# Two diagonal blocks of a Gram matrix packed in one fp32 matrix: narrower low-part products and a scaled split

## The chip, the core and the metric

One kernel runs on one core of a Trainium2 chip. The metric is the device time of one execution in microseconds (us). A core has a matrix engine (TensorE, PE in the profile), a vector engine (DVE), a scalar engine (ACT), GpSimd (POOL) and a sync engine (SP) that here only issues DMAs. Each runs its own instruction list in order; they wait for one another on semaphores.

## The reference, cut to what matters

```
text_p  = x @ W_text + b_text            # x: 4 x 2048 x 512
audio_p = ctx @ W_audio + b_audio        # ctx: 4 x 77 x 384
Q = layer_norm(text_p, g1, beta1);  K = layer_norm(audio_p, g2, beta2)
alpha = softmax(Q @ K^T / sqrt(512))
h = alpha @ audio_p @ W_out + b_out
out = layer_norm(h + x, g_out, beta_out)
```

`Q` is never formed. The scores need `x` times a matrix of 77 columns, and the variance of each row of `text_p`, which is a quadratic form `x G x^T` with the Gram matrix `G` = `W_text` (centred) times its transpose. `G` is symmetric, so only its upper block triangle is kept: block row k (128 rows) has 512 - 128k columns, with everything right of the diagonal block doubled.

## The kernel before

**Precision.** Each fp32 product that has to be exact is made of three fp32r products: high x high, high x low, low x high (`parts3`, L1080). A high part is a value rounded to fp32r, a low part the rest. `proj_hi` and `proj_lo` hold both parts of the projection matrix, once for each of 4 batches: per block row k the Gram columns, then 80 columns that are not Gram (77 scores, a linear term, a mean, one spare). The widths per block row are 592, 464, 336 and 208.

**Steps.** The 8192 rows of `x` go in 32 steps of 256 rows; step s takes batch s % 4, and each step has two tiles t = 0, 1 of 128 rows. The loops are written out on DVE, ACT and POOL, and PE and SP have the first steps written out. The PE body of a step (L1284) is: transpose tile 0 of this step into `psT`; mix tile 0 of three steps ago; project tile 0 of the previous step; mix tile 1; transpose tile 1; project tile 1, with the transposes of the probabilities in its midst. `project` (L1247) issues 3 products of 208 columns (L1258), then, at L1268, 3 of 464 (k = 1), 3 of 384 (k = 0), 3 of 336 (k = 2) and 3 of 208 (k = 3). `psT` is a single buffer: ACT rounds it to `x_hi` (L574), DVE subtracts to get `x_lo` (L806), and the next transpose waits for `x_lo_ready`. DVE's list in a step is: scores and quadratic form of tile 1 of the previous step (L908, L909), `stat_eps`, `hid` of tile 0, `x_lo` of tile 0, logits, maximum, scores and quadratic form of tile 0, `parts`, `hid` of tile 1, `x_lo` of tile 1, `inv_sum`, `sc_part`.

**Before the steps.** PE makes block row k of G in a PSUM bank (`gram`, L1125). ACT takes the high part (`t_hi`, L523), DVE the low part (`t_lo`, L767), for batch 0 only. SP copies them to batches 1 to 3 with two DMAs for each block row (`copy_gram`, L300). The same SP list then loads `x` of steps 2 and 3, places the values in `wo_hi` and `wo_lo` with 21 small SBUF-to-SBUF copies (L335), and only behind these loads `x` of step 4, whose wait is for `hid` of step 0 (L324 to L326). The second step of projections (PE body 2) is the first that waits for all Gram copies (`t_copied`, L1251).

Of the kernel before, what the change touches and what calls it, by code (L numbers as in the profile page):

```python
# [25 lines left out]
ALU = mybir.AluOpType  # L26
# [7 lines left out]
def cross_attention(nc, x, ctx, w_text, b_text, w_audio, b_audio, w_out, b_out,  # L34
# [33 lines left out]
    with ExitStack() as stack:  # L68
# [78 lines left out]

        room = [zs[:].rearrange("p b t h -> p (b t h)"), hid[:].rearrange("p c t h -> p (c t h)")]
# [14 lines left out]
        mean_of = borrow(1, P)  # L163
        mean_r = kg_hi[:, 0, 0:P]
# [34 lines left out]
        wo_hi_ready, wo_ready = sem("wo_hi_ready"), sem("wo_ready")  # L199
        val_placed = [sem(f"val_placed{q}") for q in range(B)]  # L200
# [87 lines left out]
        def _(sp):  # L288
# [84 lines left out]
        def _(pool):  # L373
# [6 lines left out]
                                    pattern=[[-1, P]], channel_multiplier=1).then_inc(ident_ready, 1)  # L380
            nc.gpsimd.memset(score_c[:, :, S:SC], 0.0).then_inc(extras_ready, 1)
# [9 lines left out]
            for k in range(KD):  # L391
                at = NX_AT[k]
                nc.gpsimd.memset(f32(proj_hi[:, :, at:at + 1]), -1.0 / D).then_inc(extras_ready, 1)
# [6 lines left out]

            pool.wait_ge(kvar_ready, 1)
# [3 lines left out]
            pool.wait_ge(extras_ready, 4 + KD)  # L405
            for k in range(KD):
                at = LIN_AT[k]
                nc.gpsimd.tensor_copy(proj_hi[:, :, at], lin[:, k:k + 1].to_broadcast([P, B])).then_inc(lin_hi_ready, 1)
            pool.wait_ge(lin_hi_ready, KD)
            for k in range(KD):  # L410
                at = LIN_AT[k]
                nc.gpsimd.tensor_tensor(proj_lo[:, :, at], lin[:, k:k + 1].to_broadcast([P, B]),
# [72 lines left out]
        def _(act):  # L485
# [34 lines left out]
            for k in range(KA):  # L520
                act.wait_ge(cxT_psum, k + 1)
                nc.scalar.activation(cxT[:, k, :], V_BANK[k][:, 0:BS], ACT.Copy).then_inc(cxT_ready, 1)
            def t_hi(k):  # L523
# [22 lines left out]
            t_hi(1)  # L546
# [5 lines left out]
            for k in range(2, KD):  # L552
                t_hi(k)
# [22 lines left out]
            def score_hi(k):  # L576
                act.wait_ge(m_psum, k + 1)
                nc.scalar.activation(proj_hi[:, :, SCORE_AT[k]:SCORE_AT[k] + S],
                                     M_BANK[k][:, 0:BS].rearrange("p (b s) -> p b s", b=B), ACT.Copy).then_inc(m_hi, 1)
# [146 lines left out]
        def _(dve):  # L726
# [40 lines left out]
            def t_lo(k):  # L767
                dve.wait_ge(g_hi, k + 1)
# [31 lines left out]
            t_lo(1)  # L800
# [22 lines left out]
            for k in range(2, KD):  # L823
                t_lo(k)
            linear(KD - 1)
            dve.wait_ge(krstd_ready, 1)
# [22 lines left out]

            dve.wait_ge(bo_loaded, 16)  # L850
# [36 lines left out]
            score_lo(3)  # L887
# [479 lines left out]
```

## Time and profile before

| what | value |
|---|---|
| median of 3 runs | 277.38 us (276.97 to 277.71) |
| the profiled execution: its own time | 277.88 us |
| its span, first to last instruction | 276.2 us |
| PE busy | 264.3 us, 96% |
| DVE busy | 230.8 us, 84% |
| POOL busy | 203.4 us, 74% |
| ACT busy | 199.1 us, 72% |
| granted TensorE clock, mean over the span | 0.992 |

The 1.7 us between the span and the time of the profiled execution lie around the first and the last instruction. Busy matmul time overlaps from one matmul to the next; the pace of PE is read from start to start.

### The profile page before, as it was taken

What the parts mean: (1) busy time and instruction counts of PE and PEld (TensorE: products, weight loads), DVE (VectorE), ACT (ScalarE), POOL (GpSimd) and SP (SyncE); (2) the same over time, 40 slices, a digit from 0 to 9 for tenths busy, and PEclk for the clock granted to TensorE, in tenths of its full rate; (3) what the DMA queues carried; (4) which work ended last, traced back from release to release, by engine and by line L of the source; (5) the groups of instructions that cost most, each with busy time, mean ns of one, the idle gap of its engine ahead of it and who ended that gap; (6) DMA issues with size and microseconds to landing.
All of it is one profiled execution on the core that took longest, in us unless ns stands there. A gap on an engine that the chain in (4) does not pass through costs nothing.

```text
span 276.2 us, 5994 instructions
## 1 busy us (share of the span) xinstructions
PE 264.3 (96%) x1705; PEld 240.3 (87%) x1705; DVE 230.8 (84%) x716; ACT 199.1 (72%) x509; POOL 203.4 (74%) x223
## 2 busy tenths in 40 slices
PE   6799999999999999999999999999999999999980
PEld 6579788999999999999999999999999999999830
DVE  3757889788888888888888888888888888888895
ACT  3584293257888887777777778888888888888881
POOL 5053400113699999999999999999999999999985
PEclk9999999999999999999999999999999999999996
DMA  6919794432244444444444444444444444454116
GB/s 188 285 53 303 277 345 159 120 105 77 77 154 152 157 152 153 154 152 153 152 153 152 152 152 153 153 152 152 152 152 154 153 152 152 152 153 148 81 77 266
DMA packets 21056, 44.03 MB, mean 159 GB/s; under 512 B 2114, under 2 KB 4750, under 8 KB 21034
## 3 DMA queue, kind: packets, MB, share of 16 engines
q1 hardware_dynamic: 20410, 42.74, 45.8%
q10 hardware_dynamic: 624, 1.06, 1.4%
q14 instruction: 16, 0.13, 0.2%
q8 instruction: 6, 0.10, 0.1%
HBM read 21.19 MB, written 16.78 MB: 138 GB/s over the span
## 4 chain that ended last, share of the span: by engine, by line
PE 86%; DVE 4%; DMA 3%; POOL 3%; ACT 2%; issue 1%; SPq 1%; POOLq 0%; ACTq 0%; DVEq 0%
PE psY L1268 44%; PE psO L1280 10%; PE psT L1193 10%; PE psY L1258 7%; DMA zs<-in_ctx_dram 3%; PE psE L1243 2%; PE psE L1244 2%; PE psY L1098 2%; PE psY L1162 1%; PE psT L1131 1%; PE psT L1162 1%; POOL zs L464 1%; POOL zs L460 1%; POOL rstd L452 1%; PE psY L1131 1%
## 5 line engine op out<-in xcount | busy, mean ns | idle before, releaser
L1268 PE MATMUL psY<-proj_hi,x_hi 128*128 128x464 f32 (+3 forms) x256 | 86.1, 336 | 0.0
L1268 PE MATMUL psY<-proj_hi,x_lo 128*128 128x464 f32 (+3 forms) x256 | 83.2, 325 | 0.0
L1268 PE MATMUL psY<-proj_lo,x_hi 128*128 128x464 f32 (+3 forms) x256 | 83.1, 325 | 0.0
L429 POOL TENSOR_TENSOR zs<-zs,shift 128x512 f32<-128x512 f32 x55 | 70.9, 1289 | 4.3
L423 POOL TENSOR_TENSOR zs<-zs,gain 128x512 f32<-128x512 f32 x55 | 71.3, 1296 | 0.9 <-ACT zs L616 0.9
L605 ACT ACTIVATE waste_act<-hid,sc 128x512 bf16<-128x512 f32 x60 | 43.4, 723 | 38.8 <-DVE hid L929 38.8
L435 POOL TENSOR_TENSOR rstd<-stat_eps,neg_half 128x4 f32<-128x4 f32 x30 | 30.5, 1017 | 40.6 <-DVE stat_eps L921 40.6
L1268 PEld LDWEIGHTS psY<-proj_lo,x_hi 128*128 128x128 f32 x256 | 48.5, 189 | 1.5
L1268 PEld LDWEIGHTS psY<-proj_hi,x_lo 128*128 128x128 f32 x256 | 48.3, 189 | 1.6
L1268 PEld LDWEIGHTS psY<-proj_hi,x_hi 128*128 128x128 f32 x256 | 48.4, 189 | 1.5
L909 DVE CUSTOM_DVE_ANT_0 waste_dve<-psY,xs,sums 128x514 bf16<-128x514 f32 x64 | 47.7, 745 | 0.2 <-issue 0.2
L616 ACT ACTIVATE zs<-hid,shift,rstd 128x512 f32<-128x512 f32 x59 | 47.5, 805 | 0.0
L929 DVE SCALAR_TENSOR_TENSOR hid<-psO,inv_sum,xs 128x512 f32<-128x512 f32 x60 | 44.8, 747 | 0.0
L806 DVE TENSOR_TENSOR x_lo<-psT,x_hi 128x512 fp32r<-128x512 f32 x64 | 43.6, 682 | 0.9 <-ACT x_hi L574 0.7
L574 ACT ACTIVATE x_hi<-psT 128x512 fp32r<-128x512 f32 x64 | 37.7, 589 | 6.7 <-PE psT L1193 6.7
L1193 PE MATMUL psT<-ident,xs 128*128 128x128 f32 x256 | 38.6, 273 | 0.0
L1193 PEld LDWEIGHTS psT<-ident,xs 128*128 128x128 f32 x256 | 29.9, 141 | 4.5 <-issue 0.4
L908 DVE TENSOR_TENSOR sc<-psY,sc_part 128x78 f32<-128x78 f32 x64 | 15.4, 240 | 21.4 <-PE psY L1268 18.1
L1280 PE MATMUL psO<-wo_hi,parts_t 128*128 128x512 f32 x60 | 26.9, 448 | 0.1
L1280 PE MATMUL psO<-wo_lo,parts_t 103*128 103x512 f32 x60 | 23.6, 394 | 0.0
L625 ACT ACTIVATE psD<-logits,neg_max 128x77 f32<-128x77 f32 x62 | 19.2, 309 | 2.2 <-DVE neg_max L941 2.2
L1258 PE MATMUL psY<-proj_hi,x_hi 128*128 128x208 f32 x64 | 19.3, 301 | 0.0
(230 smaller groups left out, 484.4 us busy)
## 6 DMA issues: line engine op xcount, KB each, us to landing
xs<-in_x_dram SPq DMA_DIRECT2D x64, 256.0 KB, 3.0
out_dram<-zs SPq DMA_DIRECT2D x29, 512.0 KB, 3.9
out_dram<-zs SPq DMA_DIRECT2D x6, 256.0 KB, 2.0
xs<-in_L_xattn_W_text_dram SPq DMA_DIRECT2D x4, 256.0 KB, 3.7
xs<-in_L_xattn_W_out_dram SPq DMA_DIRECT2D x2, 512.0 KB, 4.2
wa<-in_L_xattn_W_audio_dram SPq DMA_DIRECT2D x1, 768.0 KB, 7.8
proj_hi<-proj_hi SPq DMA_DIRECT2D x1, 768.0 KB, 8.8
proj_lo<-proj_lo SPq DMA_DIRECT2D x1, 768.0 KB, 10.7
```

The costliest lines, as they stand in the source:

```text
L423: nc.gpsimd.tensor_tensor(zs[:, q, t, :], zs[:, q, t, :], gain[:], ALU.mult).then_inc(zg_ready, 1)
L429: nc.gpsimd.tensor_tensor(zs[:, q, t, :], zs[:, q, t, :], shift[:], ALU.add).then_inc(out_ready, 1)
L574: nc.scalar.activation(x_hi[:, b % 2, t, :], psT[:], ACT.Copy).then_inc(x_hi_ready, 1)
L605: nc.scalar.activation(waste_act[:, t, :], hid[:, (b - 3) % 2, t, :], ACT.Square, bias=sc[:, q, t, S:S + 1], accum_out=stat[:, (b + 1) % B ...
L616: nc.scalar.activation(zs[:, q, t, :], hid[:, b % 2, t, :], ACT.Identity, bias=shift2[:, q, t:t + 1], scale=rstd[:, b, T + t:T + t + 1]).t ...
L806: nc.vector.tensor_tensor(x_lo[:, b % 2, t, :], psT[:], f32(x_hi[:, b % 2, t, :]), ALU.subtract).then_inc(x_lo_ready, 1)
L909: nc.vector.tensor_tensor_reduce(out=waste_dve[:, t, 0:QUAD_W], in0=psY[:, t, QUAD_AT:QUAD_AT + QUAD_W], in1=xs_rows[:, q, t, X_AT - 1:X_A ...
L929: nc.vector.scalar_tensor_tensor(hid[:, (b - 3) % 2, t, :], psO[:], inv_sum[:, q, t:t + 1], xs[:, q, t, :], ALU.mult, ALU.add).then_inc(hi ...
L1193: last = nc.tensor.transpose(psT[:, k * P:(k + 1) * P], xs[:, b, t, k * P:(k + 1) * P], ident[:])
L1258: last = nc.tensor.matmul(psY[:, t, B_AT:512], part[:, par, t, 0:P], w[:, q, 0:SW + P], start=(n == 0), stop=(n == 2))
L1268: last = nc.tensor.matmul(psY[:, t, to:to + n0], part[:, par, t, k * P:(k + 1) * P], w[:, q, at:at + n0], start=(n == 0), stop=(n == len(P ...
L1280: last = nc.tensor.matmul(psO[:], parts_t[0:rows, (b - lag) % 2, t, n, :], v[0:rows, q, :], start=(n == 0), stop=(n == 1))
```

## The change

Block rows 1 and 2 are "packed". The low part of a diagonal block is put below the diagonal of the high part's block (where a symmetric block held a mirror image), so that one 128-column product carries both. The rows are scaled first, by `rs`, so that the diagonal is exactly an fp32r value; `x_lo` of those 128 columns is then `psT * x_scale - x_hi` in place of `psT - x_hi`, and the score, linear and mean columns of block rows 1 and 2 are scaled as well. In `project`, the `x_hi` x `proj_lo` product of block row 1 has 336 columns in place of 464, that of block row 2 has 208 in place of 336.

```
@@ the projection on PE
                     to = 512 + max(k - 1, 0) * P
+                    if k in PACKED and w is proj_lo:
+                        at, n0, to = at + P, n0 - P, to + P
@@ x_lo on DVE
-                nc.vector.tensor_tensor(x_lo[:, b % 2, t, :], psT[:], f32(x_hi[:, b % 2, t, :]),
-                                        ALU.subtract).then_inc(x_lo_ready, 1)
+                nc.vector.tensor_tensor(dst[:, 0:KD:KD - 1, :], src[:, 0:KD:KD - 1, :], high[:, 0:KD:KD - 1, :], ALU.subtract)
+                for k in PACKED:
+                    last = nc.vector.scalar_tensor_tensor(dst[:, k, :], src[:, k, :], x_scale[k], high[:, k, :], ALU.mult, ALU.subtract)
+                last.then_inc(x_lo_ready, 1)
@@ DVE before the steps
+            for n, k in enumerate(PACKED):
+                nc.vector.tensor_tensor_reduce(out=waste_dve[:, n, 0:P], in0=g_raw[k][:, 0:P], in1=ident[:], scale=1.0, scalar=1e-30,
+                                               op0=ALU.mult, op1=ALU.add, accum_out=dd[:, n:n + 1]).then_inc(dg_ready, 1)
...
+            link(nc.vector.reciprocal(rec[:], dd[:]))
+            link(nc.vector.tensor_tensor(rs[:, 0:2], dd[:, 2:4], rec[:, 0:2], ALU.mult))
+            nc.vector.tensor_tensor(rs[:, 2:4], dd[:, 0:2], rec[:, 2:4], ALU.mult)
+            nc.vector.tensor_scalar(rs[:, 4:6], rs[:, 0:2], 2.0, None, ALU.mult)
+            nc.vector.tensor_scalar(rs[:, 6:8], rs[:, 0:2], -1.0 / D, None, ALU.mult).then_inc(rs_ready, 1)
...
+                if k < len(PACKED):
+                    diagonal_rest(k)
+                else:
+                    block_rest(k - len(PACKED))
...
+            dve.wait_ge(pkT_psum, 1)
+            for n, k in enumerate(PACKED):
+                nc.vector.tensor_tensor(proj_hi[:, 0, Y_AT[k]:Y_AT[k] + P], psD[:, n * P:(n + 1) * P], pk_hi[n], ALU.add).then_inc(pack_ready, 1)
@@ PE before the steps
+            pe.wait_ge(pk_ready, len(PACKED))
+            for n in range(len(PACKED)):
+                last = nc.tensor.transpose(psD[:, n * P:(n + 1) * P], pk_lo[n], ident[:])
+            last.then_inc(pkT_psum, 1)
             constant(0, C_BANK)
-            pe.wait_ge(lin_lo_ready, KD)
+            pe.wait_ge(lin_lo_ready, KD + len(PACKED))
+            pe.wait_ge(goff_ready, len(PACKED))
+            pe.wait_ge(pack_ready, len(PACKED))
@@ SP
                         if b == 2:
-                            for k in range(1, KD):
-                                copy_gram(k)
+                            copy_gram(KD - 1)
                             sp.wait_ge(wo_ready, KH)
...
                 if isinstance(i, int) and (i, b) == (0, B - 1):
+                    for k in PACKED:
+                        copy_gram(k)
                     sp.wait_ge(val_psum, len(KEYS))
```

`diagonal_rest` and `block_rest` are each one DVE instruction of 128, 128, 256 and 128 columns with a per-partition scalar. ACT takes a raw copy of block rows 1 and 2 (`g_raw`) in place of their high parts and makes the scaled high parts later, while it waited before; POOL has four more small operations at the start, two products of 128 columns, and four more columns to fill.

The list of SP before, from the loads of step 1 (rows of L326) to the values (L335):

```order
L326 DMA xs<-in_x_dram 128x512 [waits lin_ready]
L326 DMA xs<-in_x_dram 128x512
L305 DMA proj_hi<-proj_hi 128x3x384 [waits g_hi]
L305 DMA proj_lo<-proj_lo 128x3x384 [waits g_lo]
L305 DMA proj_hi<-proj_hi 128x3x256 [waits g_hi]
L305 DMA proj_lo<-proj_lo 128x3x256 [waits g_lo]
L305 DMA proj_hi<-proj_hi 128x3x128 [waits g_hi]
L305 DMA proj_lo<-proj_lo 128x3x128 [waits g_lo]
L326 DMA xs<-in_x_dram 128x512 [waits wo_ready]
L326 DMA xs<-in_x_dram 128x512 x3
L335 DMA wo_hi<-wa 77x512 [waits val_lo_ready,val_hi_ready,val_psum]
```

The same place after the change (the loads of `x` are L343 there, the Gram copies L323, the values L354):

```order
L343 DMA xs<-in_x_dram 128x512 [waits lin_ready]
L343 DMA xs<-in_x_dram 128x512
L323 DMA proj_hi<-proj_hi 128x3x128 [waits g_hi]
L323 DMA proj_lo<-proj_lo 128x3x128 [waits g_lo]
L343 DMA xs<-in_x_dram 128x512 [waits wo_ready]
L343 DMA xs<-in_x_dram 128x512 x3
L323 DMA proj_hi<-proj_hi 128x3x384 [waits pack_ready,goff_ready]
L323 DMA proj_lo<-proj_lo 128x3x256 [waits pack_ready,goff_ready]
L323 DMA proj_hi<-proj_hi 128x3x256 [waits pack_ready,goff_ready]
L323 DMA proj_lo<-proj_lo 128x3x128 [waits pack_ready,goff_ready]
L354 DMA wo_hi<-wa 77x512 [waits val_lo_ready,val_hi_ready,val_psum]
```

Four Gram copies moved behind the loads of steps 2 and 3 and now wait for `pack_ready`; the values, and all that follows them, stand behind that wait.

DVE before the steps, before the change, from `kvar` to the key scales (L828):

```order
L821 TENSOR_SCALAR kvar<-psY 52x1
L770 SCALAR_TENSOR_TENSOR proj_lo<-psD,proj_hi 128x128 [waits g_hi]
L770 SCALAR_TENSOR_TENSOR proj_lo<-psD,proj_hi 128x128
L770 SCALAR_TENSOR_TENSOR proj_lo<-psO,proj_hi 128x128 [waits g_hi]
L786 ISA waste_dve,lin<-xs,bt_rows 128x512
L786 ISA lin 128x1
L828 TENSOR_SCALAR kg_lo<-ident,krstd 128x128 [waits krstd_ready]
```

and after it:

```order
L885 ISA waste_dve,dd<-zs,ident 128x128 [waits g_raw_ready]
L885 ISA dd 128x1
L885 ISA waste_dve,dd<-zs,ident 128x128
L885 ISA dd 128x1
L826 SCALAR_TENSOR_TENSOR proj_lo<-psO,proj_hi 128x128 [waits g_hi]
L842 ISA waste_dve,lin<-xs,bt_rows 128x512
L842 ISA lin 128x1
L891 RECIPROCAL rec<-dd 128x4 [waits dh_ready,dg_ready]
L892 TENSOR_TENSOR rs<-dd,rec 128x2 [waits dve_own]
L893 TENSOR_TENSOR rs<-dd,rec 128x2 [waits dve_own]
L894 TENSOR_SCALAR rs<-rs 128x2
L895 TENSOR_SCALAR rs<-rs 128x2
```

The two low parts of block row 2 are gone from here, and two reductions and five small operations in a chain stand ahead of the key scales.

## Rows read from the trace of the kernel before

**Rows 1.** The page, part 1: busy us, share of the span, instructions.

```profile
PE 264.3 (96%) x1705; PEld 240.3 (87%) x1705; DVE 230.8 (84%) x716; ACT 199.1 (72%) x509; POOL 203.4 (74%) x223
```

**Rows 2.** Timeline, one projection on PE: start us, duration us, engine, line, what.

```profile
154.43 0.39 PE L1268 MATMUL psY<-proj_hi,x_hi 128*128 128x464 f32 x1
...
155.08 0.34 PE L1268 MATMUL psY<-proj_hi,x_hi 128*128 128x384 f32 x1
...
155.61 0.31 PE L1268 MATMUL psY<-proj_hi,x_hi 128*128 128x336 f32 x1
...
156.06 0.26 PE L1268 MATMUL psY<-proj_hi,x_hi 128*128 128x208 f32 x1
...
156.38 0.41 PE L1280 MATMUL psO<-wo_hi,parts_t 128*128 128x512 f32 x1
```

**Rows 3.** Timeline of one step, PE and DVE, from `sc` (L908) to `sc`.

```profile
153.20 0.60 PE L1193 MATMUL psT<-ident,xs 128*128 128x128 f32 x4
...
153.40 0.24 DVE L908 TENSOR_TENSOR sc<-psY,sc_part 128x78 f32<-128x78 f32 x1 [0.62 <-PE psY L1268]
...
155.12 0.68 DVE L806 TENSOR_TENSOR x_lo<-psT,x_hi 128x512 fp32r<-128x512 f32 x1
...
155.71 0.49 DVE L938 SCALAR_TENSOR_TENSOR logits<-sc,rstd,psD 128x77 f32<-128x77 f32 x2
...
158.77 0.68 DVE L806 TENSOR_TENSOR x_lo<-psT,x_hi 128x512 fp32r<-128x512 f32 x1
...
160.22 0.24 DVE L908 TENSOR_TENSOR sc<-psY,sc_part 128x78 f32<-128x78 f32 x1 [0.57 <-PE psY L1268]
```

**Rows 4.** Groups of DVE by form: count, busy us, mean ns of one, idle before.

```profile
L806 DVE TENSOR_TENSOR x_lo<-psT,x_hi 128x512 fp32r<-128x512 f32 x64 | 43.6, 682 | 0.9 <-ACT x_hi L574 0.7
...
L946 DVE RECIPROCAL inv_sum<-prob_sum 128x2 f32<-128x2 f32 x30 | 4.7, 156 | 0.0
...
L863 DVE TENSOR_TENSOR proj_lo<-psY,proj_hi 128x308 fp32r<-128x308 f32 x3 | 1.4, 458 | 0.0
...
L831 DVE SCALAR_TENSOR_TENSOR kg_lo<-ident,krstd,kg_lo 128x128 fp32r<-128x128 f32 x2 | 0.6, 334 | 0.0
...
L770 DVE SCALAR_TENSOR_TENSOR proj_lo<-psD,proj_hi 128x128 fp32r<-128x128 f32 x2 | 0.5, 273 | 0.0
```

**Rows 5.** Timeline of DVE before the first steps.

```profile
30.16 0.63 DVE L828 TENSOR_SCALAR kg_lo<-ident,krstd 128x128 fp32r<-128x128 f32 x3
...
45.96 0.46 DVE L863 TENSOR_TENSOR proj_lo<-psY,proj_hi 128x308 fp32r<-128x308 f32 x1
```

**Rows 6.** Timeline of PE: tile 0 transposed (steps 1, 4), second step's first projection.

```profile
45.54 0.66 PE L1193 MATMUL psT<-ident,xs 128*128 128x128 f32 x4
...
52.07 0.34 PE L1258 MATMUL psY<-proj_hi,x_hi 128*128 128x208 f32 x1
...
64.38 0.60 PE L1193 MATMUL psT<-ident,xs 128*128 128x128 f32 x4
```

**Rows 7.** Timeline of SP's list: start us, time of the issue us, line.

```profile
40.79 1.72 SPq L335 DMA_DIRECT2D wo_hi<-wa  x2
...
57.59 0.74 SPq L335 DMA_DIRECT2D wo_lo<-zs  x1
59.58 13.99 SPq L326 DMA_DIRECT2D xs<-in_x_dram  x5
```

**Rows 8.** Gram copies (L305): ns of an issue min/median/max; landing.

```profile
L305 SPq DMA_DIRECT2D proj_hi<-proj_hi x4: 606/987/1347, 20.6 to 35.1; - x4
...
DMA to landing us min/median/max: 3.6/5.1/10.7
```

**Rows 9.** Value copies (L335): ns of an issue min/median/max.

```profile
L335 SPq DMA_DIRECT2D wo_hi<-wa x11: 652/742/1175, 40.8 to 56.0; - x11
```

**Rows 10.** The page, part 6, loads of x: count, KB, median us to landing.

```profile
xs<-in_x_dram SPq DMA_DIRECT2D x64, 256.0 KB, 3.0
```

**Rows 11.** A stretch at the end: PE, PEld, DVE, ACT, POOL busy; granted clock; DMA.

```profile
270.00:273.00 3.00, 0.00 (x0) 0.00 (x0) 2.73 (x5) 0.69 (x2) 2.56 (x3) 0.75 0.99 391
```

More of the change, by code:

```diff
@@ L163, in cross_attention @@
         mean_of = borrow(1, P)
+        g_raw = {k: borrow(0, D - k * P) for k in PACKED}
+        pk_hi, pk_lo = [borrow(0, P) for _ in PACKED], [borrow(0, P) for _ in PACKED]
+        tri = borrow(1, P)
         mean_r = kg_hi[:, 0, 0:P]
@@ L392, in _ @@
                 at = NX_AT[k]
-                nc.gpsimd.memset(f32(proj_hi[:, :, at:at + 1]), -1.0 / D).then_inc(extras_ready, 1)
+                if k not in PACKED:
+                    nc.gpsimd.memset(f32(proj_hi[:, :, at:at + 1]), -1.0 / D).then_inc(extras_ready, 1)
             def out_lo(k):
@@ L404, in _, with column @@
             pool.wait_ge(lin_ready, KD)
[L405 to L412, printed above, removed]
+            pool.wait_ge(extras_ready, 4 + KD - len(PACKED))
+            pool.wait_ge(rs_ready, 1)
+            nc.gpsimd.tensor_tensor(lin_r[:], lin[:, 1:3], rs[:, 0:2], ALU.mult).then_inc(lin_r_ready, 1)
+            pool.wait_ge(lin_r_ready, 1)
+            def column(k):
+                return lin_r[:, PACKED.index(k):PACKED.index(k) + 1] if k in PACKED else lin[:, k:k + 1]
+            extra_columns = [(LIN_AT[k], column(k)) for k in range(KD)] + [(NX_AT[k], rs[:, 6 + n:7 + n]) for n, k in enumerate(PACKED)]
+            for at, col in extra_columns:
+                nc.gpsimd.tensor_copy(proj_hi[:, :, at], col.to_broadcast([P, B])).then_inc(lin_hi_ready, 1)
+            pool.wait_ge(lin_hi_ready, KD + 2)
+            for at, col in extra_columns:
+                nc.gpsimd.tensor_tensor(proj_lo[:, :, at], col.to_broadcast([P, B]),
                                         f32(proj_hi[:, :, at]), ALU.subtract).then_inc(lin_lo_ready, 1)
@@ L522, in _, with t_raw @@
                 nc.scalar.activation(cxT[:, k, :], V_BANK[k][:, 0:BS], ACT.Copy).then_inc(cxT_ready, 1)
+            def t_raw(k):
+                act.wait_ge(g_psum, k + 1)
+                nc.scalar.activation(g_raw[k], W_BANK[k][:, 0:D - k * P], ACT.Copy).then_inc(g_raw_ready, 1)
             def t_hi(k):
@@ L544, in _ @@
             load_row(shift, beta_out, gs_loaded)
-            t_hi(1)
+            t_raw(1)
             for k in range(KH):
@@ L551, in _ @@
                 nc.scalar.activation(KSQ[k], kT[:, k, :], ACT.Square).then_inc(ksq_ready, 1)
-            for k in range(2, KD):
-                t_hi(k)
+            t_raw(2)
+            t_hi(KD - 1)
+            act.wait_ge(dg_ready, 2)
+            nc.scalar.activation(dd[:, 2:4].bitcast(F32R), dd[:, 0:2], ACT.Copy).then_inc(dh_ready, 1)
+            act.wait_ge(rs_ready, 1)
+            act.wait_ge(pk_own, len(PACKED))
+            for n, k in enumerate(PACKED):
+                nc.scalar.activation(pk_hi[n].bitcast(F32R), pk_lo[n], ACT.Copy, scale=rs[:, 4 + n:5 + n]).then_inc(pk_hi_ready, 1)
+            for n, k in enumerate(PACKED):
+                at, w = Y_AT[k] + P, D - (k + 1) * P
+                nc.scalar.activation(proj_hi[:, 0, at:at + w], g_raw[k][:, P:P + w], ACT.Copy,
+                                     scale=rs[:, 4 + n:5 + n]).then_inc(goff_hi_ready, 1)
             def value_hi(n):
```

67 lines of the change are left out of this document (56 added, 11 removed).

## The prediction, made before the changed kernel ran

> **What bounds the kernel now.** I read the page's shares first: PE is busy 96% of the span, DVE 84%, POOL 74% [rows 1]. That alone says only who is near the limit, so I read one steady step. From one `sc` (L908) to the next are 160.22 - 153.40 = 6.82 us [rows 3]. At both, DVE had sat idle for 0.6 us until PE's projection ended: PE sets the pace, and DVE has 0.57 to 0.62 us of slack in each step. PE's cost by width, start to start [rows 2]: three products of 464 columns take 155.08 - 154.43 = 0.65 us (0.217 each), three of 336 take 0.45 (0.150), three of 208 take 0.32 (0.107).
>
> Before the first step another thing matters. SP issues 21 value copies (L335) one after the other, from 40.79 to 58.33 us, 17.54 us in all [rows 7]; an issue of them occupies SP for 0.74 us in the median and never under 0.65 [rows 9]. At 59.58 us comes the load of `x` for step 4. It lands some 3.0 us later [rows 10], 62.6, and PE transposes it at 64.38 [rows 6]: 1.8 us to spare, and no more. Whatever delays SP's list by over 1.8 us (and is not matched by a delay of PE) stops PE at step 4.
>
> **PE's saving in the steps.** In each tile one product goes from 464 to 336 columns (0.217 - 0.150 = 0.067 us) and one from 336 to 208 (0.043): 0.11 us, from the slope 0.107. I take 0.107, so 0.21 us in a step of two tiles, and 6.61 us a step if nothing else binds.
>
> **DVE's cost in the steps.** `x_lo` was one instruction of 682 ns [rows 4], 0.59 us from its start to the next one's (155.71 - 155.12) [rows 3], so about 0.08 us overlap with the next. Now there are three. The subtract of 256 columns: the slope between 308 and 512 columns is (682 - 458) / 204 = 1.1 ns a column [rows 4], so 0.40 us. The two of 128 columns with a scalar per partition: 273 ns with a constant scalar, 334 ns with one per partition [rows 4]; the second is the nearer form. The sum less three overlaps is 0.40 + 0.67 - 0.24 = 0.83 us, against 0.60: 0.23; I take 0.21 more per tile. The bounds are 0.12 (273 ns each, some rounding) and 0.30 (hardly any overlap). DVE gets 0.42 us more work in a step that becomes 0.21 us shorter, against 0.6 us of slack: nearly full.
>
> Who waits for it? The next transpose (L1193) needs `x_lo` of tile 1, since `psT` is one buffer. This closes a loop over two steps: from `sc` at 153.40, which starts when a projection ends, to the end of the second `x_lo`, 158.77 + 0.68 = 159.45, is 6.05 us; from the start of a transpose of tile 0 (153.20) to the next-but-one `sc` (160.22) is 7.02 us [rows 3]; some 0.05 us (my estimate) for the signal. Before, that is 13.12 us against two steps of PE, 13.64: the loop does not bind. After, it is 13.12 - 0.21 + 2 x 0.21 = 13.33 us, 6.67 a step, above PE's 6.61. So the step costs 6.67 us, and the saving is 0.15 us a step. With 0.12 per tile PE binds and it is 0.21; with 0.30 it is 0.06. The change stops paying in the steps at 0.36 us more per tile.
>
> The Trainium skill ("Perfetto Trace Analysis", Optimizing Scalar/DVE Operations) puts the engine-busy overhead of a DVE instruction that reads PSUM at about 125 ns. By it two more instructions cost 0.25 us per tile and the step 6.71 us, 1.2 us more over the 29 steps counted below; the nearest row here gives the figure above, and both lie inside the bounds.
>
> **What comes before the steps.** All on DVE, whose list there runs nearly without a pause up to `score_lo(3)` (L863 at 45.96) [rows 5].
> - Two reductions of 128 columns and a chain of five small operations replace two low parts ahead of the key scales (L828, at 30.16 before [rows 5]). Two low parts out, two reductions in, some 0.2 us net; the small operations take 156 ns or so each [rows 4], three of them with the wait for the one before, 0.8 us. Key scales and what PE does with them: 1.0 us later.
> - Four instructions among the low parts of `kg`: two hide in DVE's waits for ACT; those of 256 and 128 columns do not: 0.6 us.
> - Two `x_lo` at 0.21 and two scaled score parts at 0.07: 0.56 us. So `score_lo(3)` starts near 45.96 + 2.2 = 48.1.
> - Then two additions of 128 columns (0.4 us): `pack_ready` at 49.0. PE waits for that before its step 1, whose transpose began at 45.54 [rows 6]: 3.5 us later. From both sides: 2.5 (ACT and PE hide part) to 4.2.
>
> I cost ACT's and POOL's new work ahead of the steps at nothing: both engines stand idle there while DVE and PE make the key scales and, for POOL, while the high parts of `wo` are awaited. If that cover went, each would add less than 1 us.
>
> **SP's list, the term that decides.** Before, the Gram copies were issued from 31 us on, and the values from 40.79. Now four Gram copies wait for `pack_ready` at 49.0, and the value copies, and behind these the load for step 4, stand behind them. Four issues at 0.6 to 1.35 us [rows 8], taken as 0.8: 3.2 us, so values from 49.1 + 3.2 = 52.3 on. Plus 17.5 us of value issues: 69.8. Plus 3.0 us for the load: 72.8. PE's transpose of step 4 was at 64.38; it comes **8.4 us** later (7.6 with 0.6 us per Gram issue, 10 with 1.2). The 3.5 us above are inside these 8.4, not beside them. So is the wait of the second step for the last Gram copy: issued at 51.5, landing 3.6 to 5.1 us later [rows 8], 55 to 56.6, against 52.07 + 3.5 - 0.2 = 55.4 [rows 6]. The values themselves are in time: the first batch's four are issued by 55.6 and first used some 60.
>
> PE then stands idle for roughly 5 us at step 4. In a stretch of 3 us at the end without a matmul the granted clock averages 0.75, so it has dropped from 2.4 to 1.2 GHz inside it [rows 11]. How long it stays down once PE works again no row shows. Bounds: nothing, and half a step's worth lost (3.4 us). I take 2.0.
>
> **Sum.** After step 4's transpose 29 pairs of projections remain: 29 x 0.15 = 4.4 us back. 8.4 + 2.0 - 4.4 = +6.0 us. The profiled execution took 277.88 us against the median 277.38; against that median: **283.4 us**.
>
> **Rivals.**
> 1. PE keeps the whole saving (`x_lo` costs under 0.15 us more per tile): 29 x 0.21 = 6.1 back, 8.4 + 2.0 - 6.1 = +4.3, 281.7; without any clock loss 279.7. For it: the loop exceeds PE by 0.06 us only.
> 2. No stop at step 4, and the kernel is faster. Mechanism: an issue holds SP only while the queue behind it is full, so 21 value copies in a quiet stretch go out quickly and the load for step 4 leaves when `hid` of step 0 is ready. It decides if value issues average under about 0.4 us. Then only the 3.5 us remain, less the saving of 31 steps, 4.7: 276.2, or 274.3 with all of PE's saving. Against it: the lowest value issue of all is 0.65 us [rows 9], also in the stretch where little else moved. The Trainium skill ("DMA: Bandwidth & Descriptors", Anatomy of one DMA — SWDGE (gpsimd) path) puts sequencer dispatch at some 50 ns and calls descriptor generation small; that is for another path, but by it this rival would hold. The trace disagrees.
> 3. DVE becomes the bound of the steps (over 0.36 us more per tile, or 13.6 us in the loop of two steps): nothing comes back, 277.4 + 8.4 + 2.0 = 287.8. For it: DVE is nearly full, and small waits can add up. Against it: no row of 128 columns is that dear.
>
> **Chances.** Forecast 0.50; rival 1, 0.27; rival 2, 0.12; rival 3, 0.11. Changes under 0.3% (0.8 us) can't be told from none. Slower by more: 0.87; within: 0.03; faster: 0.10. The range reaches from rival 1 without a clock loss and with the short Gram issues (277.4 + 7.6 - 6.1 = 278.9) to just over rival 3, 288.5; rival 2 is left out.
>
> **What would show it.** In the changed trace: PE idle for about 5 us ahead of L1282 in step 4, released by a DMA of `x`; SP's value issues from about 52 to 70 us; `sc` to `sc` of 6.6 to 6.7 us and DVE's idle time ahead of it nearly gone; a granted clock under 1 after the stop. I am wrong if `x` for step 4 is issued by 64 us, or if the steps take 6.82 us or more.

## The result: 3.5% slower, and the profile after

Over four runs of each kernel the time went from 277.18 us (276.44 to 277.71) to 286.80 us (286.66 to 286.87): a ratio of 1.0348, 95% interval 1.0323 to 1.0374, +9.6 us. The forecast was 283.4 with a range up to 288.5, so the sign and the range held and the middle was 3.4 us short. The profiled execution took 286.85 us with a span of 285.1, 8.9 us longer than before.

Part 1 of the page after, against [rows 1]:

```profile
PE 267.7 (94%) x1707; PEld 240.8 (84%) x1707; DVE 249.4 (87%) x855; ACT 204.2 (72%) x512; POOL 206.9 (73%) x232
```

PE has fewer columns to do and is counted busy for longer: some of it ran at half clock, and in the steady steps the profile counts it as busy all the time in both kernels (68.00 us of the 68 from 174 to 242), though it has less to do in the second. DVE has 139 more instructions and 18.6 us more work.

**Where the time went before the steps were steady.** The timeline of PE after (start us, duration us, engine, line, what), first the transposes of tile 0 and tile 1 of step 1, tile 0 of step 2, then around step 4. The same instructions stood at 45.54, 48.36, 51.66, 64.38, 68.05 and 71.21 before, so [rows 6] and its neighbours shift by +2.50, +3.87, +3.75, +7.46, +8.99 and +8.88 us.

```profile
48.04 0.63 PE L1282 MATMUL psT<-ident,xs 128*128 128x128 f32 x4 [1.52 <-issue]
52.23 0.61 PE L1282 MATMUL psT<-ident,xs 128*128 128x128 f32 x4
55.41 0.66 PE L1282 MATMUL psT<-ident,xs 128*128 128x128 f32 x4
...
71.84 0.66 PE L1282 MATMUL psT<-ident,xs 128*128 128x128 f32 x4 [3.75 <-DMA xs<-in_x_dram]
...
73.47 0.63 PE L1365 MATMUL psY<-proj_hi,x_hi 128*128 128x464 f32 x1
73.89 0.48 PE L1365 MATMUL psY<-proj_lo,x_hi 128*128 128x336 f32 x1
...
77.04 0.60 PE L1282 MATMUL psT<-ident,xs 128*128 128x128 f32 x4
...
80.09 0.60 PE L1282 MATMUL psT<-ident,xs 128*128 128x128 f32 x4
```

Read it in four pieces. Step 1 starts 2.5 us later. Between 48.04 and 52.23 another 1.37 us are lost (52.23 - 48.04 = 4.19, where it was 48.36 - 45.54 = 2.82). At 71.84 PE has stood idle for 3.75 us for the load of `x` of step 4. And behind it a product of 464 columns takes 73.89 - 73.47 = 0.42 us, where it took 0.22 [rows 2]: half clock, until 76.2, for another 1.4 us. The granted clock in windows, for the kernel after. Each row has the window, its length, the busy us of PE, PEld, DVE, ACT and POOL, the granted clock (1.00 is 2.4 GHz, 0.50 is 1.2 GHz), the DMA share and GB/s:

```profile
42.00:49.00 7.00, 4.87 (x34) 3.81 (x33) 6.72 (x19) 1.80 (x5) 0.00 (x0) 0.99 0.00 2
49.00:53.00 4.00, 4.00 (x20) 3.89 (x19) 1.65 (x6) 0.42 (x2) 0.00 (x0) 0.59 1.04 355
53.00:64.00 11.00, 11.00 (x76) 10.16 (x75) 9.22 (x35) 4.55 (x12) 2.03 (x2) 1.00 0.42 123
```

and the first two of them for the kernel before:

```profile
42.00:49.00 7.00, 6.87 (x48) 5.84 (x46) 6.57 (x17) 1.88 (x4) 0.00 (x0) 1.00 0.46 140
49.00:53.00 4.00, 4.00 (x27) 3.61 (x27) 2.35 (x9) 1.20 (x2) 0.38 (x1) 1.00 0.40 115
```

PE was busy for 4.87 us of the first 7 instead of 6.87, and then ran at 1.2 GHz for most of the next 4 us. This second loss does not come with every execution. The kernel that fills the stop, below, has the same instructions as the changed one up to step 4; its profile shows a clock of 1.00 from 49 to 53 us, and 5.80 us from the transpose of step 1 to that of step 2 instead of 7.37.

The 2.5 us depend on the execution too. The kernel before and four experiments on it reach the transpose of step 1 at 44.10 to 45.86 us, the changed kernel and eight experiments on it at 47.31 to 48.68. Counted from the transpose of step 0 (35.35 before, 35.17 after) the way to step 1 grew from 10.19 to 12.87 us, by 2.7.

**SP's list after**, against [rows 7] (start us, time of the issues us):

```profile
47.70 0.61 SPq L323 DMA_DIRECT2D proj_hi<-proj_hi  x1
...
50.23 1.04 SPq L323 DMA_DIRECT2D proj_lo<-proj_lo  x1
51.38 1.73 SPq L354 DMA_DIRECT2D wo_hi<-wa  x2
...
67.95 0.74 SPq L354 DMA_DIRECT2D wo_lo<-zs  x1
68.74 17.55 SPq L343 DMA_DIRECT2D xs<-in_x_dram  x6
```

Four Gram issues from 47.70, 21 value issues from 51.38 to 68.69 (17.3 us; 17.5 before), then at 68.74 the load, which releases PE at 71.84, 3.1 us later.

**The steps.** The DVE timeline over one step after, against [rows 3]:

```profile
161.29 0.41 DVE L864 TENSOR_TENSOR x_lo<-psT,x_hi 128x256 fp32r<-128x256 f32 x1
161.62 0.60 DVE L866 SCALAR_TENSOR_TENSOR x_lo<-psT,rs,x_hi 128x128 fp32r<-128x128 f32 x2
162.14 0.15 DVE L1035 RECIPROCAL inv_sum<-prob_sum 128x2 f32<-128x2 f32 x1
162.21 0.22 DVE L989 TENSOR_TENSOR sc_part<-psY,score_c 128x78 f32<-128x78 f32 x1
162.53 0.24 DVE L997 TENSOR_TENSOR sc<-psY,sc_part 128x78 f32<-128x78 f32 x1
...
169.35 0.24 DVE L997 TENSOR_TENSOR sc<-psY,sc_part 128x78 f32<-128x78 f32 x1
```

169.35 - 162.53 = 6.82 us, just as before. `x_lo` takes 162.14 - 161.29 = 0.85 us from start to start where it took 0.59 (158.77 to 159.36), and the idle 0.57 us ahead of `sc` [rows 3] is gone. The shift is +8.9 us at step 5 and +8.9 at the end of the span: nothing comes back in the steps.

So the 8.9 us are 7.46 up to the transpose of step 4 and 1.4 of clock behind it. The changed kernel's median below is always the 286.80 above; the kernel before ran again beside each group of experiments, with medians from 277.13 to 277.57. Some of its runs there took up to 281.7 us at a mean granted clock of 0.98 to 0.99; the ratios leave out those that are over 1.5% above the fastest, and the rest widen several intervals.

The experiments ask two things: is it SP's queue alone that makes the stop, and what eats PE's saving in the steps.

### The profile page after: what moved, and what is told of

Its sections match the earlier page's. It is cut to its first block, busy times and chain, and to the rows that moved or that the text cites. A ratio compares the mean times of both kernels' runs of the same rounds, so it can differ in the third digit from the quotient of the medians.

```text
span 285.1 us, 6160 instructions
## 1 busy us (share of the span) xinstructions
PE 267.7 (94%) x1707; PEld 240.8 (84%) x1707; DVE 249.4 (87%) x855; ACT 204.2 (72%) x512; POOL 206.9 (73%) x232
## 4 chain that ended last, share of the span: by engine, by line
PE 65%; DVE 13%; SPq 8%; issue 4%; ACT 4%; DMA 3%; POOL 3%; POOLq 0%; DVEq 0%; ACTq 0%
PE psY L1365 30%; PE psO L1377 9%; PE psT L1282 8%; SPq L354 6%; PE psY L1353 5%; DMA zs<-in_ctx_dram 2%; DVE x_lo L866 2%; DVE hid L1018 2%; PE psE L1338 2%; PE psE L1339 2%; PE psY L1187 2%; DVE x_lo L864 2%; SPq L323 1%; DMA xs<-in_x_dram 1%; PE psY L1251 1%
## 5 line engine op out<-in xcount | busy, mean ns | idle before, releaser
L1365 PE MATMUL psY<-proj_hi,x_hi 128*128 128x464 f32 (+3 forms) x256 | 87.3, 341 | 0.0
L1365 PE MATMUL psY<-proj_hi,x_lo 128*128 128x464 f32 (+3 forms) x256 | 85.2, 333 | 0.0
L1365 PE MATMUL psY<-proj_lo,x_hi 128*128 128x208 f32 (+2 forms) x256 | 76.6, 299 | 0.0
L1365 PEld LDWEIGHTS psY<-proj_hi,x_lo 128*128 128x128 f32 x256 | 49.4, 193 | 1.6
L1365 PEld LDWEIGHTS psY<-proj_lo,x_hi 128*128 128x128 f32 x256 | 49.5, 193 | 1.4
L1365 PEld LDWEIGHTS psY<-proj_hi,x_hi 128*128 128x128 f32 x256 | 49.6, 194 | 0.0
L998 DVE CUSTOM_DVE_ANT_0 waste_dve<-psY,xs,sums 128x514 bf16<-128x514 f32 x64 | 47.6, 744 | 0.2 <-issue 0.2
L1282 PE MATMUL psT<-ident,xs 128*128 128x128 f32 x256 | 39.9, 278 | 5.4 <-DMA xs<-in_x_dram 3.8
L866 DVE SCALAR_TENSOR_TENSOR x_lo<-psT,rs,x_hi 128x128 fp32r<-128x128 f32 x128 | 38.4, 342 | 0.0
L864 DVE TENSOR_TENSOR x_lo<-psT,x_hi 128x256 fp32r<-128x256 f32 x64 | 26.6, 415 | 1.3 <-ACT x_hi L627 1.2
L681 ACT ACTIVATE psD<-logits,neg_max 128x77 f32<-128x77 f32 x62 | 19.8, 319 | 4.7 <-DVE neg_max L1030 2.6
```

What stands on the lines that cost most here:

```text
L864: nc.vector.tensor_tensor(dst[:, 0:KD:KD - 1, :], src[:, 0:KD:KD - 1, :], high[:, 0:KD:KD - 1, :], ALU.subtract)
L866: last = nc.vector.scalar_tensor_tensor(dst[:, k, :], src[:, k, :], x_scale[k], high[:, k, :], ALU.mult, ALU.subtract)
L998: nc.vector.tensor_tensor_reduce(out=waste_dve[:, t, 0:QUAD_W], in0=psY[:, t, QUAD_AT:QUAD_AT + QUAD_W], in1=xs_rows[:, q, t, X_AT - 1:X_A ...
L1282: last = nc.tensor.transpose(psT[:, k * P:(k + 1) * P], xs[:, b, t, k * P:(k + 1) * P], ident[:])
L1365: last = nc.tensor.matmul(psY[:, t, to:to + n0], part[:, par, t, k * P:(k + 1) * P], w[:, q, at:at + n0], start=(n == 0), stop=(n == len(P ...
```

## Experiments on the stop at step 4

**SP's order alone, in the kernel before.** Copies of block rows 1 and 2 of `G` wait for the last low part and stand ahead of the values, as in the change. The arithmetic is untouched.

```
                     sp.wait_ge(made, k + 1)
+                    if k in (1, 2):
+                        sp.wait_ge(m_lo, 4)
...
-                            for k in range(1, KD):
-                                copy_gram(k)
+                            copy_gram(KD - 1)
...
+                    for k in (1, 2):
+                        copy_gram(k)
                     sp.wait_ge(val_psum, len(KEYS))
```

> The kernel before with the four Gram copies of block rows 1 and 2 issued as in the changed kernel: behind the loads of step 3, after the last score part (46.4 us), ahead of the value copies. Nothing else. Theory: issues end near 49.8, values near 67.3, the load for step 4 lands near 70.4 instead of being there at 64.4: 6 us of stop, and 1.3 us for the clock: 284.5 us. Rival (SP's issues shrink when nothing else is going on, or the stop is absorbed by the pipeline): under 280.

Measured: 286.38 us (285.99 to 287.13). The ratio to the kernel before is 1.0299 [1.0225, 1.0373]; all ratios that follow are to the kernel before too. The waits of PE (us in total, times, longest):

```profile
PE psT L1196 <- DMA xs<-in_x_dram: 4.5, 1, 4.5
...
PE psY L1261 <- DMA proj_lo<-proj_lo: 1.4, 1, 1.4
```

The transpose of step 4 comes at 71.09 us (+6.71), that of step 5 at 79.44 (+8.23); the granted clock from 70.9 to 74.3 us is 0.50. With not one instruction of the change on PE, DVE or ACT, the order of one queue costs nearly what the whole change costs.

**The loads of step 4 placed among the values, in the changed kernel**, behind the 14th and the 18th value copy:

```
+            def load(b, i, t):
...
+                        if not (isinstance(i, int) and (i, b) == (1, 0)):
+                            load(b, i, t)
...
+                            placed += 1
+                            if placed in (14, 18):
+                                load(0, 1, placed // 18)
```

> The changed kernel; on SP's list the Gram copies stay ahead of the values, but the two loads of x for step 4 are issued after 14 and after 18 of the 21 value copies. Theory (SP's queue is the stop, the half clock its consequence): values start at 51.4, the load for step 4 leaves when hid of step 0 is ready near 63.3 and lands near 66.3, ahead of its use near 68; unlike the first SP order that was tried, the Gram copies meet no value copies on the DMA engines and land in 3.5 to 4.1 us, in time for step 2. No stop in either place, no fall of the clock: 286.8 - 3.75 - 1.35 = 281.7 us. Rival (another late thing stands behind the stop): 284 or more.

Measured: 281.95 us (281.83 to 283.38), ratio 1.0186 [1.0143, 1.023]; beside it the changed kernel's 286.80. The transpose of step 4 on PE, and the clock behind it:

```profile
68.59 0.66 PE L1290 MATMUL psT<-ident,xs 128*128 128x128 f32 x4 [0.26 <-DMA xs<-in_x_dram]
```

```profile
64.00:84.00 20.00, 19.74 (x136) 18.35 (x135) 18.90 (x68) 15.05 (x40) 10.60 (x11) 1.00 0.42 128
```

The stop is gone and with it 4.9 us, the clock loss included. What stays, a span 4.0 us over before's, is the start: the transposes of steps 2 and 3 are 4.0 us later here (55.65 and 61.54 against 51.66 and 57.58), and then no step gives anything back. This execution, too, ran at half clock at the start (0.57 from 49 to 53 us), so 1.3 of the 4.0 us are that (the shift is 2.7 at step 1 and 4.0 at step 2).

**The packed Gram copies behind the first 7 value copies, in the changed kernel:**

```
-                    for k in PACKED:
-                        copy_gram(k)
                     sp.wait_ge(val_psum, len(KEYS))
                     for n in range(len(KEYS)):
+                        if n == 1:
+                            for k in PACKED:
+                                copy_gram(k)
```

> The changed kernel, with one edit on SP's list: the four packed Gram copies are issued after the first 7 value copies instead of ahead of all 21. My theory: the stop at step 4 (PE idle 3.75 us for the load of x, then 3.4 us at half the clock, some 1.3 us lost) comes from SP's queue alone. Then the load for step 4 is issued near 63 us instead of 68.7, PE does not stop, the clock does not fall there, and the steps stay at 6.81 us, DVE-bound: 286.8 - 3.75 - 1.35 = 281.7 us. Rival (the stop only hides another late thing, such as DVE being behind): the time stays within 1 us of 286.8.

Measured: 284.54 us (282.93 to 285.65), ratio 1.02 [1.012, 1.0279]. PE's waits, and the Gram copies (L323):

```profile
PE psY L1354 <- DMA proj_lo<-proj_lo: 1.4, 1, 1.4
```

```profile
DMA to landing us min/median/max: 3.3/5.6/11.2
```

The load of step 4 leaves at 64.62 and PE no longer stops there. But the last Gram copy is issued at 51.49 instead of 50.23, and with value copies issued ahead of it it takes 5.7 us to land instead of 3.6 (median of the line 5.6; 3.8 in the changed kernel): the second step of projections now waits 1.4 us for it. I had sized the issue and left out the landing. Of the two orders, loads among the values was the better one. The profile is of the fastest of the four runs (282.93); what the others lost beyond it is not shown.

**Is the half clock behind the stop a cost of its own?** 16 products of `ident` with itself into `psT` are put ahead of the transpose of step 4 in the changed kernel, so that PE works in most of the stop.

```
+                if isinstance(i, int) and (i, b, t) == (1, 0, 0):
+                    wait_if_positive(pe, x_lo_ready, T, i, T * b + t)
+                    keep_busy(16, psT)
```

> The changed kernel with 16 matmuls of the identity (results overwritten) on PE in the stop of step 4, after x_lo_ready and ahead of the wait for x. The stop stays at some 3.8 us. Clock theory: the granted clock stays at 1.0 behind the stop, and the 1.3 us lost after it come back: 285.5 us. Rival (the 1.3 us are the pipeline refilling, whatever the clock): 286.8 us, with the clock at 1.0.

Measured: 285.57 us (285.16 to 286.07), 1.2 under the changed kernel, ratio to before 1.022 [1.015, 1.0291]. The window around the stop:

```profile
67.00:84.00 17.00, 15.49 (x113) 14.51 (x112) 11.21 (x42) 9.40 (x26) 7.07 (x8) 1.00 0.33 102
```

The clock stays full, and from the arrival of `x` to the second `sc` behind it are 79.36 - 72.44 = 6.92 us instead of 80.29 - 71.84 = 8.45: 1.5 us. The clock is a cost of its own beside the stop. In this profile the start ran at full clock too, which brought PE to the stop earlier. SP's list was not earlier (the load left at 69.21), so PE had to stand there longer: the two gains do not add up.

## Experiments on the steps

**The narrower products alone, in the kernel before.** The two low products are 128 columns narrower and nothing else changes; the low parts of two diagonal blocks are left out of the result.

```
+                    if k in (1, 2) and w is proj_lo:
+                        at, n0, to = at + P, n0 - P, to + P
```

> The kernel before with the two low products 128 columns narrower and nothing else (the low parts of two diagonal blocks are left out). Theory: PE-bound steps fall from 6.82 to 6.61 us, 31 of them: 277.2 - 6.5 = 270.7 us. Rival (DVE's or another engine's loop ends the saving early): more than 272.5.

Measured: 273.46 us (271.9 to 274.96), ratio 0.9831 [0.9745, 0.9917]: 3.9 us less, not the 6.5 of PE's whole saving. The four runs fall in two pairs, near 272.1 and near 274.8; the profile is of the lowest. In it a step takes 6.68 us in the mean, not 6.61, though DVE still has idle time; over 31 steps that is some 4.4 us less than before. The timeline at a place where PE is held up, ACT and then PE:

```profile
196.00 0.58 ACT L639 ACTIVATE parts_t<-psE 128x512 fp32r<-128x512 f32 x1
```

```profile
196.22 0.60 PE L1193 MATMUL psT<-ident,xs 128*128 128x128 f32 x4
196.72 0.49 PE L1282 MATMUL psO<-wo_hi,parts_t 128*128 128x512 f32 x1
```

The mix starts 0.50 us behind the transpose, where 0.36 is usual (160.02 to 160.38 before): it waits for `parts_t`, the rounded transposed probabilities, which ACT has finished at 196.58, 0.14 us before. The timeline puts no releaser beside so short a wait. ACT does `parts_t` only behind the square of `hid` (L605), and that waits for `hid` of tile 1, late in DVE's list. This closes a loop of two steps that I had not seen: `sc`, DVE's list to `hid` of tile 1, square, `parts_t`, mix, projection, `sc`. Its rows in the kernel before:

```profile
159.61 0.58 ACT L639 ACTIVATE parts_t<-psE 128x512 fp32r<-128x512 f32 x1
...
160.38 0.48 PE L1280 MATMUL psO<-wo_hi,parts_t 128*128 128x512 f32 x1
...
167.05 0.24 DVE L908 TENSOR_TENSOR sc<-psY,sc_part 128x78 f32<-128x78 f32 x1 [0.57 <-PE psY L1268]
```

There `parts_t` ends at 160.19, 6.79 us behind the `sc` at 153.40; I take 0.13 for the signal; and from the mix at 160.38 to the `sc` at 167.05 are 6.67. The sum, 13.59 us, is within 0.05 of two steps of PE (13.64). Less the 0.21 that the narrower products save in it, it is 13.38, 6.69 a step, and 6.68 was measured.

**The same with `parts_t` ahead of the square on ACT:**

```
+                if live(2):
+                    parts_out(b, i)
                 if live(3):
                     square(b, i, 1)
-                if live(2):
-                    parts_out(b, i)
```

> The kernel before with narrower low products alone, and on ACT the copy of the transposed probabilities (parts_t) ahead of the square of tile 1. With narrower products alone the steps took 6.68 us, not the 6.61 of PE's products. Theory: a loop over two steps closes through parts_t: sc, hid of tile 1, square, parts_t, mix of tile 0, projection, sc; 6.79 + 0.13 + 6.67 = 13.59 us before, less 0.21 = 13.38, 6.69 a step. Without the square in the loop PE's products bind: 6.61 us a step, 2 us less than the 273.5 of the narrower products alone: 271.5. Rival (POOL, whose own work is 6.4 to 6.6 us a step, holds the pace at 6.68): no change, 273.5.

Measured: 270.94 us (270.54 to 271.55), ratio 0.978 [0.9749, 0.9812], 6.2 us under before. DVE, `sc` to `sc`:

```profile
195.36 0.24 DVE L908 TENSOR_TENSOR sc<-psY,sc_part 128x78 f32<-128x78 f32 x1 [0.37 <-PE psY L1270]
...
202.00 0.24 DVE L908 TENSOR_TENSOR sc<-psY,sc_part 128x78 f32<-128x78 f32 x1 [0.37 <-PE psY L1270]
```

6.64 us (6.63 over many steps): close to PE's pace of 6.61 by the prediction's slope of 0.107 per tile. The loop through ACT was real. It is worth 0.05 us a step, 1.4 us, which is what the two profiled executions differ by (271.90 and 270.54); the 2.5 us between the medians hold the spread of the kernel above as well. The low parts of the diagonal blocks are missing here too.

**Three instructions for `x_lo`, in the kernel before**, as in the change but with a scale of 1.0, so that the result is the same.

```
-                nc.vector.tensor_tensor(x_lo[:, b % 2, t, :], psT[:], f32(x_hi[:, b % 2, t, :]),
-                                        ALU.subtract).then_inc(x_lo_ready, 1)
...
+                nc.vector.tensor_tensor(dst[:, 0:KD:KD - 1, :], src[:, 0:KD:KD - 1, :], high[:, 0:KD:KD - 1, :], ALU.subtract)
+                for k in (1, 2):
+                    last = nc.vector.scalar_tensor_tensor(dst[:, k, :], src[:, k, :], one_col[:, 0:1], high[:, k, :], ALU.mult, ALU.subtract)
```

> The kernel before with x_lo as three instructions (scale 1.0 from a per-partition column), products as before. DVE's own work would be 6.36 us a step (6.82 less 0.46 idle: of the 0.57 us shown as idle some 0.11 is DVE's own wait on sc_part) plus 2 x 0.25 less a wait for ACT of 0.07: 6.81, just under PE's 6.82. Theory: no measurable change, 277.2 to 277.7 us, with DVE's idle time ahead of the scores of tile 1 gone. Rival (the loop over two steps through psT binds): 6.85 or more, over 278 us.

Measured: 279.08 us (278.8 to 279.62), ratio 1.0036 [0.9964, 1.0107]. The interval does not settle it; the trace does: steps of 6.88 us instead of 6.82, 1.9 us over 31 of them, so the slack ahead of `sc` was less than the 0.50 us added. DVE's list would give 6.36 + 0.50 = 6.86 (its 6.36 are worked out below), the loop through ACT (13.59 + 0.25) / 2 = 6.92. This run does not tell the two apart. For the loop speaks that `sc` still waits for PE in about every second step (10 times, 2.4 us in all, from 100 to 242 us), which DVE's list as the only bound would not leave.

**One subtraction for `x_lo`, in the changed kernel** (the low part of `x` is then not scaled, which the result would need):

```
-                nc.vector.tensor_tensor(dst[:, 0:KD:KD - 1, :], src[:, 0:KD:KD - 1, :], high[:, 0:KD:KD - 1, :], ALU.subtract)
-                for k in PACKED:
-                    last = nc.vector.scalar_tensor_tensor(dst[:, k, :], src[:, k, :], x_scale[k], high[:, k, :], ALU.mult, ALU.subtract)
+                last = nc.vector.tensor_tensor(x_lo[:, b % 2, t, :], psT[:], f32(x_hi[:, b % 2, t, :]), ALU.subtract)
```

> The changed kernel with x_lo again as one subtraction of 512 columns (the scaling of the low part of x is left out). My theory: the three instructions fill DVE, which sets the pace of 6.81 us. Then the steps become PE-bound at 6.61 to 6.63 us and some 27 of them give back 5.2 us, and the stop at step 4 stays: 281.5 us. Rival (PE's narrower products do not save 0.21 us, and PE is the bound at 6.8): no change, 286.8 less 0.3.

Measured: 282.93 us (281.95 to 283.06), ratio 1.013 [1.0062, 1.0198]: 3.9 under the changed kernel. Steps of 6.68 us, as in the kernel with the narrower products alone. So the two extra instructions per tile take back all that the narrower products had gained in the steps (6.82 to 6.68). The rest of the gap to what I expected is the stop. PE's wait for the load of `x` (us in total, times, longest):

```profile
PE psT L1280 <- DMA xs<-in_x_dram: 5.2, 1, 5.2
```

PE comes to it earlier, waits 5.2 us instead of 3.75, and the clock is at half from 68.1 to 74.9.

**Both of these together** (SP's order with Gram copies behind 7 values, and one subtraction):

> Both edits of the two runs above together: what is left of the cost is the longer way to the first projection alone. If the three terms (stop at step 4 with its clock, DVE's pace, late start) are independent: 286.8 - 5.1 - 5.3 = 276.4 us, about the kernel before. If the stop hides part of the DVE cost, more is left, 278.

```
-                    for k in PACKED:
-                        copy_gram(k)
...
                     for n in range(len(KEYS)):
+                        if n == 1:
+                            for k in PACKED:
+                                copy_gram(k)
...
+                last = nc.vector.tensor_tensor(x_lo[:, b % 2, t, :], psT[:], f32(x_hi[:, b % 2, t, :]), ALU.subtract)
```

Measured: 281.45 us over ten runs (279.92 to 284.05), ratio 1.012 [1.007, 1.0169], 5 us off. PE's waits:

```profile
PE psY L1352 <- DMA proj_lo<-proj_lo: 3.0, 1, 3.0
```

The wait for the last Gram copy in step 2, 1.4 us with SP's order alone, is 3.0 us here, and half clock from 56.9 to 63.7 followed. What PE gains ahead of a fixed arrival only lengthens its wait there.

**ACT's order in the changed kernel.** The same edit as above (`parts_t` ahead of the square). If the loop through ACT held the changed kernel, it should gain; if DVE's list did, not.

> The changed kernel with the same reordering on ACT alone. Two things could hold its steps at 6.81 us: the loop through parts_t (13.38 + 0.25 over two steps: 6.82) or DVE's own list, which has no idle time. Loop theory: the steps fall to 6.65 and the time to 282.5. DVE theory: the steps stay at 6.79 to 6.81, 286.3 to 286.8 us. I expect the second.

Measured: 286.94 us (286.32 to 287.22), ratio 1.0346 [1.0312, 1.038]. ACT's wait ahead of `parts_t` shows that it is early now:

```profile
ACT parts_t L695 <- PE psE L1339: 25.2, 31, 1.3
```

Steps of 6.79 us, 0.02 less. So DVE's list alone holds the pace as well, and from 161 to 242 us the changed kernel's profile names no wait of DVE for another engine. By the sum: before, DVE ran 6.36 us (6.82 - 0.46, worked out below) in a step of 6.82; 0.50 for two `x_lo`, less 0.06 for a wait for ACT that is no longer there, is 6.80.

**DVE's order too.** With ACT's edit, both `sc_part` (L989) are taken one instruction forward, so that `sc` does not stand right behind the instruction whose result it waits for (0.1 us from the end of `sc_part` to `sc` each time: 162.43 to 162.53).

```
@@ logits of both tiles
+                if live(1):
+                    part_of_scores(b, i, 0)
                 wait_if_positive(dve, logits_ready, T, i, T * (b - 2) + T)
@@ end of the step
+                if live(1):
+                    part_of_scores(b, i, 1)
                 if live(2):
                     inverse_sum(b, i)
-                if live(1):
-                    part_of_scores(b, i, 1)
```

> The changed kernel with the ACT reordering, and on DVE two operations moved so that no operation waits for the one right ahead of it: sc_part of tile 0 before the maximum, sc_part of tile 1 before inv_sum. No work is taken away. DVE theory: some 0.1 us of own wait goes in each of the two places, DVE's list takes 6.6 us, PE's products bind: 6.62 us a step, 27 steps, 5 us: 281.8. Rival (another loop, through psT or POOL, stands close behind): 6.70 a step, 284.

Measured: 286.24 us (285.41 to 287.12), ratio 1.0315 [1.0279, 1.0351]. The expectation was missed by 4.4 us. A new wait stands in the steps:

```profile
DVE parts L1041 <- ACT parts L689: 10.9, 29, 0.4
```

`sc_part` now stands ahead of `neg_max`, so `neg_max` is 0.15 us later, with it ACT's exponentials and its rounding (L689), and DVE waits 0.38 us for these ahead of `parts`. That this wait is what keeps the steps from 6.62 us is read from the trace; no run took it away. Steps of 6.76 us instead of 6.82: 0.06 less. In the profiled execution PE also stood 5.7 us at step 4 for the load, not 3.75, and the clock was at half until 77.8 us: the start ran at full clock, and PE came there earlier.

**Everything that keeps the result** (this one and the loads among the values):

> The changed kernel with all three reorderings: loads of x for step 4 between the value copies, parts_t ahead of the square on ACT, the two sc_part moved on DVE. If the terms add: 286.8 - 5.1 (stop and clock) - 5 (steps of 6.62 us) = 276.7 us, 0.5 us under the kernel before (277.2); what is left of the cost is the first projection 3.7 us later, of the gain 0.2 us in each of some 30 steps. Rival (with the stop gone, DVE's start-up delay shows as a wait elsewhere): over 278.

Measured: 281.21 us (279.86 to 284.91) over six runs, before 277.54 beside it, ratio 1.0131 [1.01, 1.0162]. Without the longest run the median is 280.83. What is left of the stop at step 4:

```profile
PE psT L1293 <- DMA xs<-in_x_dram: 1.3, 1, 1.3
```

The steps take 6.76 us. It is some 6 us better than the change (5.6 by the medians) and still 3.7 us worse than the kernel before. In the profile, whose start ran at full clock, the transpose of step 2 comes 2.2 us later than before and that of step 4, with the wait for its load, 3.5 us later; the steps return 1.7 us at most.

## Why the prediction was right, and which step of it failed

**SP's queue: right.** The load for step 4 stands behind four Gram issues and 21 value issues. Forecast for the transpose of step 4: +8.4 us; measured +7.46. The terms: the first addition done near 47.6 us and the second at 47.8, not 49.0; Gram issues 3.7 us, not 3.2; value issues 17.3, not 17.5; load 3.1, not 3.0. The kernel before with this order alone shows the mechanism with nothing else in it (+6.71 us at this place).

**The start of step 1: inside its bounds.** +2.5 us against 3.5 (2.5 to 4.2) in this pair of profiles, 2.7 counted from step 0. What I had not counted is the clock there: +1.37 us more by the next transpose, in those executions in which it falls. In the changed kernel both lie inside the 7.46; in the kernel with the loads among the values they are the 4.0 us that remain.

**The clock behind the stop: right in kind.** 2.0 us forecast, between 0 and 3.4. Measured are 1.3 to 1.5 by the shift of the next transposes (8.88 - 7.46 and 8.99 - 7.46), and 1.5 by the kernel that fills the stop.

**Rival 2 fell as its price said.** The value issues average 17.3 / 21 = 0.82 us, twice its point of decision. The figure of the Trainium skill ("DMA: Bandwidth & Descriptors", Anatomy of one DMA — SWDGE (gpsimd) path), some 50 ns of dispatch, is for another path and does not describe this queue.

**The saving of 0.15 us a step: the step that failed.** The steps take 6.82 us after as before, which is rival 3's pace and one of the two signs by which the prediction said it would be wrong; 4.4 us did not come back. Three things in it were off. `x_lo` costs 0.25 us more per tile, not 0.21 (342 ns for the 128-column form, 415 for the 256 columns). The rule of the Trainium skill ("Perfetto Trace Analysis", Optimizing Scalar/DVE Operations), some 125 ns for a DVE instruction that reads PSUM, would give 0.25 for two more instructions, and from start to start the trace agrees (0.60 to 0.85). The slack of 0.57 us that I read from [rows 3] included DVE's own wait: `sc` would have stood 0.1 us behind `sc_part` in any case, so 0.46 was real, less than the 0.50 added. And the loop that I priced, through `psT`, was not the tightest: by it a step would be (13.12 - 0.21 + 0.50) / 2 = 6.71 us; the one through `parts_t` gives (13.38 + 0.25) / 2 = 6.815. Rival 3's point was put at 0.36 us more per tile. DVE's list of 6.36 - 0.06 us plus twice that cost reaches 6.82 at 0.26, and so does the loop, 13.38 plus once that cost, at 13.64. So nothing comes back in the steps from 0.26 us per tile on, and `x_lo` cost 0.25.

So the sum 8.4 + 2.0 - 4.4 = 6.0 should have read 7.5 + 1.4 - 0 = 8.9 (of the span; +9.6 between the medians). Two terms were too high, by 1.5 us together, and the third gave back 4.4 that never came. That the forecast lay only 3.4 us short is in part luck: the errors had opposite signs, and the range held because it had been drawn to just over rival 3. The time that rival 3 gave (287.8) was the nearest of all; its mechanism, DVE's list as the bound, is borne out by the kernel with ACT's order changed (though at 0.25 us per tile and not at the 0.36 that it named), and its chance of 0.11 was too small.

## What to carry to other kernels

Before a wait is put into a DMA queue, list what is queued behind it and when the first consumer of each needs it; behind such a wait a load with 1.8 us to spare is late, and here it was better to move that load forward among the small copies (281.95 us) than to move the Gram copies (284.54). When an engine's idle time is to be filled, subtract first the part that is its own latency between two dependent instructions, and follow every loop through the other engines over two steps: one with 0.05 us of slack, which no wait of PE in the profile named, held the narrower products at 6.68 us a step instead of 6.63. An edit that only makes an engine arrive earlier at a transfer whose time is fixed buys nothing there, and can cost the clock.

## What the runs showed of the hardware

The granted clock fell to 1.2 GHz behind a stop of PE: of 3.75 us in the changed kernel, of 4.5 us in the kernel before with SP's order changed, where it averages 0.50 from 70.9 to 74.3 us. It cost 1.3 to 1.5 us there. It also fell at the start of the steps, but not in every execution. Four profiles have it below full speed from 49 to 53 us (the changed kernel, and those with the loads among the values, with the Gram copies behind 7 values, and with ACT's order changed), with PE busy for 4.87 to 4.89 of the 7 us from 42 on. In three others with almost the same idle time it stayed at 1.00: the kernel that fills the stop (4.76 of 7), the one with ACT's and DVE's order changed (4.86), and the last one (4.75). The same idle time, and the same code, do not always bring it down; what decides it no run here shows.

SP took 0.65 to 1.3 us for each of the 21 small copies from SBUF to SBUF, before and after the change. The four late Gram copies landed 3.4 to 4.2 us behind their issue in the changed kernel, and 5.5 to 5.7 us with seven value copies issued ahead of them. One DVE instruction that needs the result of the one right before it started 0.1 us after that one's end (162.43 to 162.53), where independent ones start before the end of the one ahead (161.62, 0.08 us before 161.29 + 0.41).
